# Landmark attention outputs: written out over the images, operands read where they lie, inverse and projection multiplied once per image

## The reference

```
qkv = (x @ w_qkv).reshape(B, N, 3, H, D)
Q, K, V = qkv[0] / scale, qkv[1], qkv[2]          # after a transpose
K_lm = K.reshape(B, H, L, segs, D).mean(axis=-2)  # 16 landmarks per head
Q_lm = Q.reshape(B, H, L, segs, D).mean(axis=-2)
kernel1 = softmax(Q @ K_lm^T)                     # 1024 x 16 per head
kernel2 = softmax(Q_lm @ K_lm^T)                  # 16 x 16
kernel3 = softmax(Q_lm @ K^T)                     # 16 x 1024
SV = kernel1 @ iterative_inv(kernel2) @ (kernel3 @ V)
out = SV @ w_proj + b_proj + V                    # added to x
```

## Time and profile before

| what | us |
|---|---|
| time, median of 3 runs | 6689.68 (6679.41 to 6699.53) |
| profiled execution: span from first to last instruction | 6691.7 |
| TensorE busy in the span | 5796.7 (87%) |
| VectorE busy | 3550.5 (53%) |
| ScalarE busy | 2484.9 (37%) |
| GpSimd busy | 2461.4 (37%) |

### The profile page before, as it was taken

How to read it: one execution, slowest core, us unless ns; L and a number is a source line. 1 busy time by engine, 2 the same in 40 slices (tenths; PEclk the granted TensorE clock), 3 DMA queues, 4 the chain that set the end, 5 groups by cost and what they waited for, 6 DMA issues and landing times. The chain is left out here.

```text
span 6691.7 us, 128834 instructions
## 1 busy us (share of the span) xinstructions
PE 5796.7 (87%) x44140; PEld 3230.3 (48%) x44140; DVE 3550.5 (53%) x5261; ACT 2484.9 (37%) x3334; POOL 2461.4 (37%) x2361
## 2 busy tenths in 40 slices
PE   8579999999978976668677879999999997889996
PEld 6553333333353344447565653333333335878885
DVE  4247777777746964434544446666666663441212
ACT  2225555555522212223222225555555552112221
POOL 0046556555513951110000045555555541053023
PEclk9789999999988987778757989999999998979998
DMA  4853344434324220000001453333333335667665
GB/s 147 257 178 88 92 95 92 93 92 93 89 66 138 89 59 9 0 1 1 1 0 31 116 175 106 105 107 106 108 106 106 107 99 198 195 233 237 209 225 186
DMA packets 839802, 741.85 MB, mean 111 GB/s; under 512 B 514933, under 2 KB 722454, under 8 KB 828727
## 3 DMA queue, kind: packets, MB, share of 16 engines
q1 hardware_dynamic: 827062, 710.76, 36.3%
q0 software_dynamic: 12288, 25.18, 1.1%
HBM read 463.94 MB, written 278.00 MB: 111 GB/s over the span
## 5 line engine op out<-in xcount | busy, mean ns | idle before, releaser
L1186 DVE TENSOR_REDUCE L3B_nmax<-L3B_R 128x1 bf16<-128x1024 f32 x768 | 941.1, 1227 | 635.0 <-PE L3B_R L1080 635.0
L1186 DVE TENSOR_REDUCE L0B_nmax<-L0B_R 128x1 bf16<-128x1024 f32 x768 | 937.3, 1223 | 390.5 <-PE L0B_R L1080 375.6
L1172 ACT ACTIVATE L0B_PT<-L0B_R 128x1024 f32<-128x1024 f32 x768 | 785.2, 1023 | 671.4 <-PE L0B_R L1090 642.3
L1172 ACT ACTIVATE L3B_PT<-L3B_R 128x1024 f32<-128x1024 f32 x768 | 753.5, 1022 | 575.7 <-PE L3B_R L1090 575.4
L1090 PE MATMUL L0B_R<-L0B_QS,L0B_KS 64*128 64x512 bf16 (+1 forms) x6144 | 806.4, 383 | 42.5 <-issue 36.1
L1116 PE MATMUL L3B_O<-L3B_PT,L3B_VA 128*64 128x512 f32 x3072 | 743.7, 605 | 0.0
L1090 PE MATMUL L3B_R<-L3B_QS,L3B_KS 64*128 64x512 bf16 (+1 forms) x6144 | 730.7, 377 | 2.8 <-DVE L3B_nmax L1186 2.8
L1090 PEld LDWEIGHTS L0B_R<-L0B_QS,L0B_KS 64*128 64x128 bf16 (+1 forms) x6144 | 261.2, 95 | 510.1 <-issue 210.6
L1090 PEld LDWEIGHTS L3B_R<-L3B_QS,L3B_KS 64*128 64x128 bf16 (+1 forms) x6144 | 299.6, 94 | 329.3 <-ACT L3B_PT L1172 5.7
L1111 PE MATMUL L0B_O<-L0B_PT,L0B_VA 128*32 128x256 f32 x6144 | 420.7, 391 | 2.5 <-issue 2.2
L1116 PEld LDWEIGHTS L3B_O<-L3B_PT,L3B_VA 128*64 128x64 f32 x3072 | 186.5, 136 | 371.1 <-issue 371.1
(11 more groups left out here) (406 smaller groups left out, 9182.6 us busy)
## 6 DMA issues: line engine op xcount, KB each, us to landing
L3F_weights<-in_L3F_w SPq DMA_DIRECT2D x79, 1251.0 KB, 5.8
scr_sumsL<-L3B_OT SPq DMA_DIRECT2D x96, 512.0 KB
L3C_sums<-scr_sumsL SPq DMA_DIRECT2D x96, 512.0 KB, 9.7
scr_rel<-L0R_terms SPq DMA_DIRECT2D x64, 384.0 KB
L0B_raw<-scr_rel SPq DMA_DIRECT2D x192, 128.0 KB
L3B_raw<-scr_rel SPq DMA_DIRECT2D x384, 64.0 KB
scr_parts<-L0B_qk_parts SPq DMA_DIRECT2D x96, 224.0 KB, 2.3
scr_parts<-L3B_qk_parts SPq DMA_DIRECT2D x96, 224.0 KB, 2.2
```

The lines of the kernel that those rows point to most:

```text
L1172: nc.scalar.activation(PT[:, (8 * u + j) % NPT, :, :], score_pair(u, j), ACT.Exp).then_inc(s_exp, 1)
L1186: nc.vector.tensor_reduce(nmax[:, u % 2, 4 * t:4 * t + 1], pair.rearrange("p j n -> p (j n)"), AX, ALU.max, negate=True).then_inc(s_mx, 1)
```

## The change

In landmark_inverse the last product swaps its operands, so that the transpose of M2 comes out. In landmark_outputs the hardware loop becomes a Python loop, written out for the 8 images. The matmuls read QT, BK and M2T in place, so the three copies go. M2T is multiplied with the projection once for each image into MW (two matmuls, one copy by ScalarE), and the turned kernel1 is multiplied with MW directly; the product of 512 columns and svT go. Two tiles share a bank of products and one add of 384 columns. E, k1T and MW have two buffers each, PSUM is split into 4 banks of scores, 2 of turned blocks (copied by ScalarE alone) and 2 of products. The queues of the engines interleave the images: the scores of image b+1 stand between the transposes and the products of image b.

The core of the diff (the semaphores' declarations and the removed bodies, which the listing above shows, are cut):

```diff
-                product(6, c, VT, T3)
+                product(6, c, T3, VT)
...
-                nc.scalar.copy(chunk(M2, c), out(6, c)).then_inc(s_a, 1)
+                nc.scalar.copy(chunk(M2T, c), out(6, c)).then_inc(s_a, 1)
...
+    SC = 4
+        score = st.ps("scores", [P, SC, 512])
+        turned = st.ps("turned", [CG, 2, 512])
+        outs = st.ps("outs", [P, 2, 512])
+        MW = [st.sb(f"MW{i}", [CG, G, C]) for i in range(2)]
+        E_ = [st.sb(f"E{i}", [P, SC, 2 * C]) for i in range(2)]
+        k1T = [st.sb(f"k1T{i}", [CG, G, HW]) for i in range(2)]
...
         @block.tensor
         def _(pe):
+            def scores(b):
+                for n in range(SC):
+                    pos(pe, s_sub, SC * (b - 1) + n + 1)
+                    for q in range(2):
+                        t = 2 * n + q
+                        for k in range(G):
+                            mm = nc.tensor.matmul(score[:, n, q * C + k * CG:q * C + (k + 1) * CG],
+                                                  QT[:, G * b + k, t * P:(t + 1) * P], BKall[:, G * b + k, :], start=True, stop=True)
+                    mm.then_inc(s_sc, 1)
+
+            def weights(b):
+                pos(pe, s_add, 4 * b)
+                for k in range(G):
+                    mm = nc.tensor.matmul(outs[0:CG, 0, k * C:(k + 1) * C], M2T[:, G * b + k, :], wp[:, k, :], start=True, stop=True)
+                mm.then_inc(s_mw, 1)
+
+            def turn(b):
+                for f in range(2):
+                    pe.wait_ge(s_k1, SC * b + 2 * f + 2)
+                    for k in range(G):
+                        pos(pe, s_tc, 4 * b + 2 * f + k - 1)
+                        for q in range(4):
+                            t = 4 * f + q
+                            mm = nc.tensor.transpose(turned[:, k, q * P:(q + 1) * P],
+                                                     E_[b % 2][:, t // 2, t % 2 * C + k * CG:t % 2 * C + (k + 1) * CG], cst["ident"][:, :])
+                        mm.then_inc(s_tn, 1)
+
+            def products(b):
+                for n in range(4):
+                    if n == 0:
+                        pe.wait_ge(s_mc, b + 1)
+                    pos(pe, s_add, 4 * b + n - 1)
+                    pe.wait_ge(s_tc, 4 * b + 2 * (n // 2) + 2)
+                    for q in range(2):
+                        t = 2 * n + q
+                        for k in range(G):
+                            mm = nc.tensor.matmul(outs[:, n % 2, q * C:(q + 1) * C], k1T[b % 2][:, k, t * P:(t + 1) * P], MW[b % 2][:, k, :],
+                                                  start=(k == 0), stop=(k == 1))
+                    mm.then_inc(s_out, 1)
+
+            scores(0)
+            pe.wait_ge(s_w, 16)
+            for b in range(B):
+                weights(b)
+                turn(b)
+                if b + 1 < B:
+                    scores(b + 1)
+                products(b)
 
         @block.scalar
         def _(act):
...
+            exps(0)
+            for b in range(B):
+                act.wait_ge(s_mw, b + 1)
+                nc.scalar.copy(MW[b % 2][:, :, :], outs[0:CG, 0, 0:2 * C].rearrange("p (k n) -> p k n", k=G)).then_inc(s_mc, 1)
+                for f in range(2):
+                    for k in range(G):
+                        act.wait_ge(s_tn, 4 * b + 2 * f + k + 1)
+                        nc.scalar.copy(k1T[b % 2][:, k, f * 512:(f + 1) * 512], turned[:, k, :]).then_inc(s_tc, 1)
+                if b + 1 < B:
+                    exps(b + 1)
 
         @block.vector
         def _(dve):
...
+            def add(b):
                 for n in range(4):
+                    dve.wait_ge(s_out, 4 * b + n + 1)
+                    xt = X[:, b * T + 2 * n:b * T + 2 * n + 2, :]
+                    nc.vector.tensor_tensor(xt, xt, outs[:, n % 2, 0:2 * C].rearrange("p (t c) -> p t c", t=2), ALU.add).then_inc(s_add, 1)
+
+            shift(0)
+            sums(0)
+            for b in range(B):
+                if b + 1 < B:
+                    shift(b + 1)
+                add(b)
+                if b + 1 < B:
+                    sums(b + 1)
```

More of the change, by code:

```diff
@@ L1976, in _, with landmark_inverse @@
             image(B - 1, True)
-def landmark_inverse(nc, K2, T3, M2, cst):
+def landmark_inverse(nc, K2, T3, M2T, cst):
     NC_, GC, ITER = 4, NGRP // 4, 6
@@ L2094, in _, with landmark_outputs @@
                                                        in1=bc(eyes[:, e, :], 1, GC), op0=ALU.mult, op1=ALU.add).then_inc(s_d, 1)
-def landmark_outputs(nc, X, QT, BKall, M2, cst, Wp):
-    J = 20
+def landmark_outputs(nc, X, QT, BKall, M2T, cst, Wp):
+    SC = 4
     with Stage(nc, "L2C") as st:
-        ring = st.ps("ring", [P, 8, 512])
-        q2 = st.sb("q2", [CG, G, HW])
-        B2, Ms = st.sb("B2", [CG, G, CG]), st.sb("Ms", [CG, G, CG])
+        score = st.ps("scores", [P, SC, 512])
+        turned = st.ps("turned", [CG, 2, 512])
+        outs = st.ps("outs", [P, 2, 512])
         wp = st.sb("wp", [CG, G, C])
-        E_ = st.sb("E", [P, 4, 2 * C])
-        mx, sm = st.sb("mx", [P, 4, 24]), st.sb("sm", [P, 4, 24])
-        k1T, svT = st.sb("k1T", [CG, G, HW]), st.sb("svT", [CG, G, HW])
+        MW = [st.sb(f"MW{i}", [CG, G, C]) for i in range(2)]
+        E_ = [st.sb(f"E{i}", [P, SC, 2 * C]) for i in range(2)]
+        mx, sm = st.sb("mx", [P, SC, 24]), st.sb("sm", [P, SC, 24])
+        k1T = [st.sb(f"k1T{i}", [CG, G, HW]) for i in range(2)]
         s_w = st.sem("weights_loaded")
-        s_op = st.sem("operands_copied")
-        s_pass = st.sem("pool_wait_passed")
-        filled = st.sem("bank_filled")
+        s_sc = st.sem("scores_ready")
         s_mx = st.sem("max_taken")
@@ L2114, in landmark_outputs, with pos, heads @@
         s_exp = st.sem("probs_ready")
-        s_sm = st.sem("sums_taken")
+        s_sm = st.sem("sums_step")
         s_k1 = st.sem("kernel1_ready")
-        s_tr = [st.sem("copied_scalar"), st.sem("copied_vector")]
-        s_add = st.sem("tile_added")
-        block = st.block()
+        s_tn = st.sem("kernel1_turned")
+        s_tc = st.sem("turned_copied")
+        s_mw = st.sem("weights_product")
+        s_mc = st.sem("weights_copied")
+        s_out = st.sem("pair_product")
+        s_add = st.sem("pair_added")
+        block = st.block()
+        def pos(eng, s, v):
+            if v > 0:
+                eng.wait_ge(s, v)
+        def heads(x):
+            return x.rearrange("p (h l) -> p h l", l=LM)
         @block.sync
@@ L2143, in _ @@
                         for k in range(G):
[L2144 to L2162, removed]
-                    for k in range(G):
-                        mm = nc.tensor.matmul(ring[:, (12 + t) % 8, 0:C], svT[:, k, t * P:(t + 1) * P], wp[:, k, :],
-                                              start=(k == 0), stop=(k == 1))
-                    mm.then_inc(filled, 1)
+                            mm = nc.tensor.matmul(score[:, n, q * C + k * CG:q * C + (k + 1) * CG],
+                                                  QT[:, G * b + k, t * P:(t + 1) * P], BKall[:, G * b + k, :], start=True, stop=True)
@@ L2168, in _, with exps @@
+            scores(0)
[6 more added lines that the diff above has]
+                products(b)
         @block.scalar
         def _(act):
[L2170 to L2178, removed]
+            def exps(b):
+                for n in range(SC):
+                    act.wait_ge(s_sub, SC * b + n + 1)
+                    nc.scalar.activation(E_[b % 2][:, n, :], E_[b % 2][:, n, :], ACT.Exp).then_inc(s_exp, 1)
@@ L2180, in _ @@
         @block.vector
         def _(dve):
-            with dve.Fori(0, B) as b:
-                for n in range(4):
[L2184 to L2204, removed]
@@ new lines, in shift @@
+            def shift(b):
+                for n in range(SC):
+                    dve.wait_ge(s_sc, SC * b + n + 1)
+                    s = heads(score[:, n, 0:2 * C])
+                    nc.vector.tensor_reduce(mx[:, n, :], s, AX, ALU.max).then_inc(s_mx, 1)
+                    dve.wait_ge(s_mx, SC * b + n + 1)
+                    if n == 0:
+                        pos(dve, s_tn, 4 * (b - 1))
+                    nc.vector.tensor_tensor(heads(E_[b % 2][:, n, :]), s, mx[:, n, :].to_broadcast([P, 24, LM]),
+                                            ALU.subtract).then_inc(s_sub, 1)
@@ new lines, in sums @@
+            def sums(b):
+                for n in range(SC):
+                    dve.wait_ge(s_exp, SC * b + n + 1)
+                    pos(dve, s_k1, SC * (b - 1) + n + 1)
+                    nc.vector.tensor_reduce(sm[:, n, :], heads(E_[b % 2][:, n, :]), AX, ALU.add).then_inc(s_sm, 1)
+                    dve.wait_ge(s_sm, 2 * (SC * b + n) + 1)
+                    nc.vector.reciprocal(sm[:, n, :], sm[:, n, :]).then_inc(s_sm, 1)
+                    dve.wait_ge(s_sm, 2 * (SC * b + n) + 2)
+                    e = heads(E_[b % 2][:, n, :])
+                    nc.vector.tensor_tensor(e, e, sm[:, n, :].to_broadcast([P, 24, LM]), ALU.mult).then_inc(s_k1, 1)
```

(6 more changed lines are left out.)

## The result

The changed kernel took 6644.5 us (median of five, 6635.8 to 6653.4) against 6689.7: a ratio of 0.9932, interval 0.9910 to 0.9953, 45 us faster. The forecast was 6632, in a range of 6604 to 6658.

The account below looks back on a forecast made before the run. The outputs' stage was taken as a chain through the engines, 28.2 us an image. Start to 3122.1, seven turns of 20.9 and an end of 9.4 gave 3277.7 instead of 3334.9: gain 57.2, 6632 us, range 6604 to 6658.

Parts of the forecast that it names:

- Loop and terms: Landmark outputs: a turn per image is handoff 0.05, half the transposes 1.87, scores 5.89, products 6.72, add 0.71, sums 5.65: 20.9 us.
- Removed steps: Landmark outputs, per image: query copy and its rest, two GpSimd copies, 512-column matmuls with the inverse and four result copies go.
- The clock: TensorE's clock level in the outputs, called the unknown: scores between 3.81 and 7.14 us, products between 5.44 and 8.00.
- the likeliest case: Landmark outputs with the clock mixed: scores 5.89, products 6.72, gain 57.2 us, 6632 us for the median; chance 0.62.
- scores always cold, products started cold: Rival for the outputs' loop: scores 7.14, products 8.00, a turn of 23.4 us, gain 37, 6653 us; chance 0.17.
- the forecast's own range: Whole kernel's time if the clock in the landmark outputs is mixed: 6616 to 6645 us; chance 0.62.
- transposes in a row raised the clock: Argument against cold scores, from the stage after the outputs: clock 0.50 during thirteen of sixteen transposes, 0.98 at their end.
- loss of 2.56 us for a cold start: Taken from the inverse: its first 32 two-pass instructions took 5.44 us, later ones 2.88.
- bound of 8.00 for the products: Outputs' products, per image: 8.00 us as upper end when started cold, 5.44 as lower end.
- no other stage moves by more than a few us: Stages outside the change: the prediction counts as wrong if another one moves by more than a few us.
- Slower by code fetch: Rival: fetching the eight written-out image copies stalls TensorE; gain gone from 7.2 us an image, 6712 at 10 us; chance 0.03.
- The gain is mostly removed steps and little overlap: Landmark outputs: if the shift waited until after the adds, only 30 us would return in seven turns, giving 6661.

Follow-up runs that it names:

- first rest filled: Useless matmuls (two of 512 columns) behind the weights' product alone, none between the halves of the transposes, added to the changed kernel: 6629.6 us in one run.

## Why the prediction was right, and where it was off

- **Loop and terms: right.** From the end of the first image's sums (3120.52) to the end of the last one's (3279.60) there are seven turns of 22.7 us. Sums 5.65 (3183.65 to 3189.30), handoff 0.05, the add of 384 columns 0.554 against 0.56 taken, the weights' product and its copy hidden, the sums at once behind the adds.
- **Removed steps: right.** No burst of 512 columns, no rest for the queries. Copying them again cost 1.99 us a turn before the clock's share.
- **The clock: mis-sized, and with it the likeliest case.** The step that failed reads: "I take the middle, 6.72: the scores now stand where the matmuls with the inverse stood, right behind the transposes, where the clock used to rise". What stood there were matmuls of 512 columns. The scores did not raise it: 6.98 us in all seven turns for 5.89 forecast, and products of 62.5 / 8 = 7.81 for 6.72. That is 2.2 us a turn, less 0.4 in the other terms, 1.8 x 7 = 13 us. In the loop this is the rival "scores always cold, products started cold" (a turn of 23.4, 6653), which had 0.17. The start (1.6 us earlier, the first scores warm) and the end (0.5 us) gave 2 back: 46.4 us gained in the stage for 57.2 forecast and 37 by that rival. That the time still falls into the forecast's own range, 6616 to 6645, by half a us, is partly the luck of that first image.
- **What was read wrongly for it.** Against that rival stood that transposes in a row raised the clock. The row does not show it: sixteen matmul instructions of 192 columns ran at 0.50 for 5.45 us up to 0.90 us ahead of those transposes, and of the eight bursts of sixteen in that stage, five stayed at 0.50 for their whole 3.62 us, the one behind a long rest among them. What raised the clock in the other three is open. And the loss of 2.56 us for a cold start was only a part: the next 32 in the inverse still took 3.61 instead of 2.88, 3.29 us in all. So the bound of 8.00 for the products was too low; four of the eight took 8.21 to 8.75. From the kernel before:

```profile
3009.32 3.61 PE L2023 MATMUL L2B_ps<-L2B_K2T,L2B_V 96*96 96x96 f32 x32
...
3347.10 3.62 PE L102 MATMUL L2F_ring<-ident,L2F_tok 128*96 128x128 f32 x16 [12.69 <-DVE L2F_tok L155]
...
3373.53 5.45 PE L2285 MATMUL L2F_ring<-L2F_wu,L2F_fT 32*128 32x192 f32 x16 [1.35 <-DVE L2F_fT L2357]
3379.88 3.40 PE L102 MATMUL L2F_ring<-ident,L2F_tok 128*96 128x128 f32 x16 [0.90 <-DVE X L2361]
```

- **Between stage and whole.** The span fell by 40.8, the stage by 46.4. Up to the end of the last attention stage the lead held (48.6 us at its last matmul, which starts at 5568.6 and 5520.0). Of the 7.8 lost after it, 5.9 lie in the gate's matmuls of the last stage, which the change does not touch: 57.6 us instead of 51.7, at a mean clock of 0.62 instead of 0.70. The experts' output matmuls behind them lasted the same, 667.6 and 667.7. Executions differ by more there (70.1 us with the first rest filled), so nothing ties it to the change; why the clock differs was not tried. My claim that no other stage moves by more than a few us was just missed.
- **Slower by code fetch: no.** The one rest of TensorE's matmuls on its own queue is the 1.24 us at the stage's start; the rests inside the turns end with a tile of VectorE's.
- **"The gain is mostly removed steps and little overlap": right in sign, too mild.** Without overlap the stage was 19 us shorter than with it.

The sixteen transposes of a turn, split by a rest of 0.84 to 1.71 us, never raised the clock in the changed kernel: it was 0.50 at their end in all eight images. In the kernel before, in five of the eight images, it rose within 0.8 us of the start of the matmuls of 512 columns (in the fourth 0.50 from 3215.24 to 3215.62, 1.00 from 3215.70) and 2.0 to 3.4 us after it in the other three, so whether these or the transposes ahead of them raised it there is open. Nor is it the transposes alone that put the scores at the low level: with the rests filled, eight transposes took 1.08 us at 1.00, and the scores behind them 3.71.

## What to carry to other kernels

On TensorE ask of every burst at which clock it will start: what stands ahead of it, and which rest lies between. Here the burst of loads and short matmuls took 3.71 us straight behind the products and 6.98 behind the transposes with their rests, and the stage with that overlap was 19 us longer than without any; put ahead of the transposes, straight behind the products and beside VectorE's sums, the same burst took 3.71 and the stage 116.9 us instead of 179.0. An order of queues is an overlap only if the loop through the engines gets shorter: draw the loop, and see which step leaves it.

## What the runs showed of the hardware

- Every burst of scores (32 weight loads of 128 columns, matmuls of 96) that began at 0.50 stayed there for its whole length: in three images before (7.13 to 7.14 us, where the second image's took 3.81 at 1.00), in all seven turns after (6.98); with the adds between the shifts 45 of them stayed there for 9.1 us without a rest. In the changed kernel the clock rose within the products in all eight images, 2.2 to 6.8 us after their start.
- Scores that begin at 1.00 straight behind products kept it (3.71 us) in all seven later images without overlap and in all six turns with the scores first. Behind a rest they lost it within the burst in some: 1.8 to 2.0 us in behind one of 2.16 (the last four images before), 0.7 us in behind a rest of 1.71 (sixth turn, first rest filled), 0.2 to 1.8 us in behind one of 1.99 (seven images, queries copied again).
- The rests cost more than their own length: seven rests of 1.99 us for a copy, 14 us, became 27 us over eight images, and filling the two rests of a turn (1.89 to 1.90 us, 3.87 in the first image, and 0.84 to 1.71) with 3.3 us of useless matmuls won 48.5 us in the stage.
- Executions with the same code in a stage ran it at different levels: the gate's 192 matmuls of the last stage lasted 51.5 to 70.1 us, from their first to their last start, at mean clocks of 0.70 to 0.50. A difference of times is put down to a change only after the changed stage's own length.
